# One layer's expert attention: the pair-matrix products of two tiles taken at once, and the copies around them moved

## What is computed

```python
gate_v = _get_sel_gate(x, sel_v_w, rs)      # sigmoid of logits, the best 2 of 8, normalised
gate_o = _get_sel_gate(x, sel_o_w, rs)
q = jnp.einsum('bsd,hpd->bhsp', x, q_w.reshape(H, P, D))
k = jnp.einsum('bsd,hpd->bhsp', x, k_w.reshape(H, P, D))
xv = jnp.einsum('bsd,hedp->bshep', x, v_w.reshape(H, E, D, P))
v = jnp.einsum('bshep,bshe->bhsp', xv, gate_v)
att = jax.nn.softmax(jnp.einsum('bhqp,bhkp->bhqk', q, k) * SCALE, axis=-1)
ctx = jnp.einsum('bhqk,bhkp->bqhp', att, v)
weighted = ctx[:, :, :, None, :] * gate_o[..., None]
out = jnp.einsum('bshep,hepd->bsd', weighted, o_w.reshape(H, E, P, D))
```

## Time and profile before

| what | value |
|---|---|
| median of 3 runs | 3170.46 us (3169.66 to 3173.8) |
| profiled execution, device time | 3168.74 us |
| its span | 3167.0 us |
| PE busy | 2907.0 us, 92% |
| DVE busy | 2780.7 us, 88% |
| ACT busy | 2341.8 us, 74% |
| POOL busy | 2322.8 us, 73% |
| chain that ended last | PE 59%, of it 46% in the units (L2221) and 3% in the pair products (L2254) |

### The profile page before, as it was taken

How to read it: one execution, slowest core, us unless ns; L and a number is a source line. 1 busy time by engine, 2 the same in 40 slices (tenths; PEclk the granted TensorE clock), 3 DMA queues, 4 the chain that set the end, 5 groups by cost and what they waited for, 6 DMA issues and landing times.

```text
span 3167.0 us, 78218 instructions
## 1 busy us (share of the span) xinstructions
PE 2907.0 (92%) x24620; PEld 2176.0 (69%) x24620; DVE 2780.7 (88%) x9085; ACT 2341.8 (74%) x7546; POOL 2322.8 (73%) x3112
## 2 busy tenths in 40 slices
PE   7489992897689996999999999999999999999998
PEld 7257762675357774677777777777777777777776
DVE  6789997899989986888888888898898898898897
ACT  4866668888976665777777777777777777777776
POOL 2799994666876662677777777777777777777777
PEclk8589995898789997999999999999999999999999
DMA  4000000220000004100000000000000000000000
GB/s 131 8 2 2 2 2 18 68 75 13 1 6 16 16 16 109 30 9 8 7 9 8 7 9 8 7 9 8 7 9 8 8 9 8 7 9 8 7 8 6
DMA packets 114508, 55.31 MB, mean 17 GB/s; under 512 B 18352, under 2 KB 113712, under 8 KB 114096
## 3 DMA queue, kind: packets, MB, share of 16 engines
q1 hardware_dynamic: 114096, 50.30, 5.8%
HBM read 41.81 MB, written 8.45 MB: 16 GB/s over the span
## 4 chain that ended last, share of the span: by engine, by line
PE 59%; DVE 1%; ACT 1%; POOL 1%; DMA 0%; issue 0%; SPq 0%; POOLq 0%; ACTq 0%; DVEq 0%
PE ps_sw_a L2221 24%; PE ps_sw_d L2221 22%; PE ps_sw_w L2267 4%; PE ps_sw_w L2254 3%; PE ps_sw_s L2236 2%; PE ps_sw_s L2278 2%; PE ps_sw_m L2243 1%; ACT sw_scaled L1962 0%; DVE sw_v_part L2117 0%; PE ps_sw_m L2229 0%; DMA sw_v<-in_L_ffn_v_w 0%; POOL sw_v_pair L1889 0%; DVE sw_v_low L2056 0%; DVE sw_o_low L2063 0%; ACT sw_v_high L2017 0%
## 5 line engine op out<-in xcount | busy, mean ns | idle before, releaser
L1962 ACT ACTIVATE sw_scaled<-ps_sw_a,sw_gate_o 128x128 f32<-128x128 f32 x2048 | 620.3, 447 | 254.1 <-PE ps_sw_a L2221 247.0
L1962 ACT ACTIVATE sw_scaled<-ps_sw_a,sw_gate_v 128x128 f32<-128x128 f32 x2048 | 597.3, 448 | 196.2 <-PE ps_sw_a L2221 194.4
L2117 DVE SCALAR_TENSOR_TENSOR sw_o_part<-ps_sw_d,sw_gate_o,sw_o_part 128x128 f32<-128x128 f32 x1920 | 555.6, 339 | 63.1 <-PE ps_sw_d L2221 60.5
L1889 POOL TENSOR_TENSOR sw_v_pair<-sw_v_part,sw_scaled 128x256 f32<-128x256 f32 x512 | 381.9, 746 | 157.0 <-DVE sw_v_part L2117 91.6
L2117 DVE SCALAR_TENSOR_TENSOR sw_v_part<-ps_sw_d,sw_gate_v,sw_scaled 128x128 f32<-128x128 f32 x1024 | 303.9, 337 | 126.1 <-PE ps_sw_d L2221 107.1
L1915 POOL TENSOR_TENSOR sw_o_rest<-sw_o_rest,sw_scaled 128x256 f32<-128x256 f32 x384 | 285.4, 743 | 158.0 <-ACT sw_scaled L1962 120.7
L2117 DVE SCALAR_TENSOR_TENSOR sw_v_part<-ps_sw_d,sw_gate_v,sw_v_part 128x128 f32<-128x128 f32 x1024 | 304.8, 339 | 0.0
L1918 POOL TENSOR_TENSOR sw_o_rest<-sw_o_rest,sw_scaled 128x256 f32<-128x256 f32 x384 | 282.6, 736 | 30.1
L1894 POOL TENSOR_TENSOR sw_v<-sw_v_pair 128x128 f32<-128x128 f32 x512 | 244.6, 478 | 40.1
L1014 POOL TENSOR_TENSOR at_key_wide<-at_keyT,c_half_heads 128x1024 f32<-128x1024 f32 x128 | 242.6, 1895 | 4.6 <-ACT at_keyT L1112 4.6
L2221 PE MATMUL ps_sw_a<-sw_v_high,sw_xT_high 128*128 128x512 f32 x512 | 234.5, 458 | 8.2 <-DVE sw_v_low L2056 8.2
(11 more groups left out here) (337 smaller groups left out, 8511.3 us busy)
## 6 DMA issues: line engine op xcount, KB each, us to landing
re_values<-in_ctx SPq DMA_DIRECT2D x128, 64.0 KB, 2.4
l_ctx<-in_ctx SPq DMA_DIRECT2D x16, 256.0 KB, 4.5
x<-in_x SPq DMA_DIRECT2D x16, 256.0 KB, 4.6
re_ctx<-in_ctx SPq DMA_DIRECT2D x16, 256.0 KB, 3.1
scratch_x<-x SPq DMA_DIRECT2D x64, 64.0 KB, 1.5
sw_x<-scratch_x SPq DMA_DIRECT2D x64, 64.0 KB, 1.9
sw_x_res<-scratch_x SPq DMA_DIRECT2D x64, 64.0 KB, 1.8
out<-sw_y SPq DMA_DIRECT2D x64, 64.0 KB, 1.5
```

Source lines behind the costliest of these rows:

```text
L1889: pool.tensor_tensor(v_pair[:, h % 2], v_part[:, h], scaled[:, h % 4, 2:4], ALU.add)\
L1962: act.activation(scaled[:, h % 4, e], ps_a[h % 2][:, e], ACT.Copy, scale=gates[:, s, h, HALF_E + e:HALF_E + e + 1]).then_inc(a_scaled[kind ...
L2117: dve.scalar_tensor_tensor(out=acc[:, e % 2], in0=ps_d[h % 2][:, e], scalar=gates[:, s, h, e:e + 1], in1=before, op0=ALU.mult, op1=ALU.add ...
```

## The change

- `pair_keys` now handles two tiles at once: the moving operand is 256 columns, `xT` of an even tile and of the next. `xT` holds 4 tiles and `uT` two. The step runs for even tiles only (`of_pair`). Of its four groups of two heads, groups 0 and 1 (`pair_keys(0)`, lag 2) come at the end of an iteration, groups 2 and 3 (`pair_keys(2)`, lag 3) between v4 and v5. Nothing of it is left between v5 and v6.
- The copies `keep_u` are four, each of 512 columns, for even tiles only; they follow v2, v3, v5 and v6.
- `xT_high` is made from `xT` in SBUF by a step of its own, `round_x`, with lag 3; `keep_x` keeps lag 1.
- All other lags of what follows grow by two (units v from 2 to 4, units o from 3 to 5, logits, route, scores and exp from 1 to 3, store from 4 to 6). `round_v`, `low_v`, `round_o`, `low_o` and the fetches of the weights keep theirs.
- The steps of `route` write over their inputs, and `place` is one row of 8 values read for all 16 groups.

```diff
-xT = k.sb("sw_xT", [P, 2, P])
+xT = k.sb("sw_xT", [P, 4, P])
...
-uT = k.sb("sw_uT", [P, SH, P])
+uT = k.sb("sw_uT", [P, SH, 2, P])
...
-place = k.sb("sw_place", [P, 2 * SH, SE])
+place = k.sb("sw_place", [P, SE])
...
-r = {n: k.sb("sw_r_" + n, G) for n in ("plus", "p", "eq1", "w1", "sel1", "p2", "eq2", "w2", "sel2", "sel")}
+r = {n: k.sb("sw_r_" + n, G) for n in ("equal", "sel", "p2")}
...
+def of_pair(step):
+    def at(i, s, rd):
+        if i % 2 == 0:
+            step(i, s, rd)
+    return at
...
     def _(sp):
...
-        sp.dma_start(place[:], A["c_place"].rearrange("p (g e) -> p g e", e=SE)).then_inc(q["place"], 16)
+        sp.dma_start(place[:], A["c_place"][:, 0:SE]).then_inc(q["place"], 16)
...
         def tile_in(dst, i):
...
-        straight([(0, fetch), (1, only_first(fetch_v)), (1, only_first(fetch_o(0, 4))), (2, fetch_residual),
-                  (2, only_first(fetch_o(4, 10))), (3, only_first(fetch_o(10, 16))), (4, store)])
+        straight([(0, fetch), (1, only_first(fetch_v)), (1, only_first(fetch_o(0, 4))), (4, fetch_residual),
+                  (2, only_first(fetch_o(4, 10))), (3, only_first(fetch_o(10, 16))), (6, store)])
...
-            pool.tensor_tensor(xT_low[:, s], xT[:, s], xT_high[:, s].bitcast(F32), ALU.subtract)\
+            pool.tensor_tensor(xT_low[:, s], xT[:, i % 4], xT_high[:, s].bitcast(F32), ALU.subtract)\
...
         def add_v(h):
...
-        stages = [(2, add_v(0)), (2, add_v(1)), (1, low_x), (4, finish)] + [(2, add_v(h)) for h in range(2, SH)]
-        stages += [(3, add_o(h)) for h in range(6)] + [(0, rstd)] + [(3, add_o(h)) for h in range(6, SH)]
+        stages = [(4, add_v(0)), (4, add_v(1)), (3, low_x), (6, finish)] + [(4, add_v(h)) for h in range(2, SH)]
+        stages += [(5, add_o(h)) for h in range(6)] + [(0, rstd)] + [(5, add_o(h)) for h in range(6, SH)]
...
         def keep_x(i, s, rd):
...
+            if not first(i, 4):
+                act.wait_ge(q["scores"], i - 3)
+                act.wait_ge(q["xT_low"], i - 3)
+            act.activation(xT[:, i % 4], ps_m[:, 0], ACT.Copy).then_inc(q["xT"], 1)
+        def round_x(i, s, rd):
+            act.wait_ge(q["xT"], i + 1)
...
-                act.wait_ge(q["scores"], i - 1)
...
-            act.activation(xT[:, s], ps_m[:, 0], ACT.Copy).then_inc(q["xT"], 1)
-            act.activation(xT_high[:, s], ps_m[:, 0], ACT.Copy).then_inc(q["xT_high"], 1)
+            act.activation(xT_high[:, s], xT[:, i % 4], ACT.Copy).then_inc(q["xT_high"], 1)
...
         def keep_probs(i, s, rd):
...
         def keep_u(n):
             def step(i, s, rd):
...
-                if n == 0 and not first(i, 1):
+                if n == 0 and i:
...
-                act.activation(uT[:, 4 * n:4 * n + 4], ps_w[n].rearrange("p (h t) -> p h t", h=4), ACT.Copy)\
-                    .then_inc(q["uT"], 1)
-            return step
+                act.activation(uT[:, 2 * n:2 * n + 2], ps_w[n % 2].rearrange("p (h c t) -> p h c t", h=2, c=2),
+                               ACT.Copy).then_inc(q["uT"], 1)
+            return of_pair(step)
...
         def keep_ctx(b):
             def step(i, s, rd):
...
-        exps = [(1, lambda i, s, rd, lo=lo: exp_scores(i, s, rd, lo)) for lo in range(0, SH, 2)]
-        vs, os = ([(lag, scale(kind, h)) for h in range(SH)] for kind, lag in (("v", 2), ("o", 3)))
-        stages = vs[:2] + [(1, keep_x)] + vs[2:4] + [(1, exp_logits), (2, keep_probs)] + vs[4:6]
-        stages += [(1, keep_u(0)), vs[6], (1, keep_u(1)), vs[7]] + os[:3] + [(2, keep_ctx(0)), os[3], exps[0]]
-        stages += [os[4], (2, keep_ctx(1)), os[5], exps[1], os[6], exps[2], os[7], exps[3]]
+        exps = [(3, lambda i, s, rd, lo=lo: exp_scores(i, s, rd, lo)) for lo in range(0, SH, 2)]
+        vs, os = ([(lag, scale(kind, h)) for h in range(SH)] for kind, lag in (("v", 4), ("o", 5)))
+        stages = vs[:2] + [(1, keep_x), (3, round_x), vs[2], (3, keep_u(0)), vs[3], (3, keep_u(1)), (3, exp_logits), (4, keep_probs)]
+        stages += [vs[4], vs[5], (3, keep_u(2)), vs[6], (3, keep_u(3)), vs[7]] + os[:3]
+        stages += [(4, keep_ctx(0)), os[3], exps[0], os[4], (4, keep_ctx(1)), os[5], exps[1], os[6], exps[2], os[7], exps[3]]
...
             def step(i, s, rd):
+                p = decays
...
-                    lambda: dve.tensor_scalar(r["plus"][:], decays[:], 1.0, None, ALU.add),
-                    lambda: dve.reciprocal(r["p"][:], r["plus"][:]),
...
+                    lambda: dve.tensor_scalar(p[:], decays[:], 1.0, None, ALU.add),
+                    lambda: dve.reciprocal(p[:], p[:]),
+                    lambda: dve.tensor_reduce(rm["m1"][:], p[:], AX.X, ALU.max),
+                    lambda: dve.tensor_tensor(r["equal"][:], p[:], wide(rm["m1"][:]), ALU.is_equal),
+                    lambda: dve.tensor_tensor(r["equal"][:], r["equal"][:], place[:].unsqueeze(1).broadcast_to(G), ALU.mult),
...
-                 for kind, lag in (("v", 2), ("o", 3)) for h in range(SH)}
-        R = [[(1, route(n))] for n in range(RANK)]
+                 for kind, lag in (("v", 4), ("o", 5)) for h in range(SH)}
+        R = [[(3, route(n))] for n in range(RANK)]
...
-            "v": [[], [], [(2, sums(0))], [(2, sums(1))], [(2, sums(2))], [], *R[0:5], R[5] + R[6], R[7],
+            "v": [[], [], [(4, sums(0))], [(4, sums(1))], [(4, sums(2))], [], *R[0:5], R[5] + R[6], R[7],
...
-            "o": [R[12], R[13] + R[14], R[15] + R[16], [(1, peak)], [(1, shifts)], R[17], R[18],
-                  [(2, low_ctx(0))], [(0, front(0))], R[19] + [(0, front(1))], [(0, front(2))],
-                  [(2, low_ctx(1))], [], [], [], []],
+            "o": [R[12], R[13] + R[14], R[15] + R[16], [(3, peak)], [(3, shifts)], R[17], R[18],
+                  [(4, low_ctx(0))], [(0, front(0))], R[19] + [(0, front(1))], [(0, front(2))],
+                  [(4, low_ctx(1))], [], [], [], []],
...
         def turn_x(i, s, rd):
...
-            if not first(i, 1):
-                pe.wait_ge(q["decays"], i)
+            if i >= 1:
+                pe.wait_ge(q["xT"], i)
+            if i >= 3:
+                pe.wait_ge(q["decays"], i - 2)
...
         def turn_probs(i, s, rd, lo):
...
         def logits(i, s, rd):
...
-            pe.wait_ge(q["xT_high"], i + 1)
-            pe.matmul(ps_m[:, 1], xT[:, s], W["sel"][:], start=True, stop=True).then_inc(q["logits"], 1)
-        def pair_keys(n):
+            pe.wait_ge(q["xT"], min(i + 3, TILES))
+            pe.matmul(ps_m[:, 1], xT[:, i % 4], W["sel"][:], start=True, stop=True).then_inc(q["logits"], 1)
+        def pair_keys(lo):
             def step(i, s, rd):
-                if i == 0:
-                    pe.wait_ge(prep["kept"], 2 + n)
-                elif not first(i, 2):
-                    pe.wait_ge(q["ctx_low"], 2 * (i - 2) + n + 1)
-                else:
-                    pe.wait_ge(q["uT"], 1 + n)
-                for h in range(4):
-                    m = pe.matmul(ps_w[n][:, h * P:(h + 1) * P], W["pair"][:, 4 * n + h], xT[:, s],
-                                  start=True, stop=True)
-                m.then_inc(q["u"], 1)
-            return step
+                if lo == 0:
+                    pe.wait_ge(q["xT"], i + 2)
+                for n in (lo, lo + 1):
+                    if n >= 2:
+                        pe.wait_ge(q["uT"], 2 * i + n - 1)
+                    elif i == 0:
+                        pe.wait_ge(prep["kept"], 3)
+                    else:
+                        pe.wait_ge(q["ctx_low"], 2 * (i - 2) + n + 1)
+                    both = xT[:, i % 4:i % 4 + 2].rearrange("p c t -> p (c t)")
+                    for h in range(2):
+                        m = pe.matmul(ps_w[n % 2][:, 2 * h * P:2 * (h + 1) * P], W["pair"][:, 2 * n + h], both,
+                                      start=True, stop=True)
+                    m.then_inc(q["u"], 1)
+            return of_pair(step)
...
         def context(i, s, rd):
-            upto = min(i + 2, TILES) if isinstance(i, int) else i + 2
-            wait_alone(pe, (q["v"], SH * i + SH), (q["p_kept"], i + 1), (q["uT"], 2 * upto))
-            if isinstance(i, int) and i == TILES - 1:
+            wait_alone(pe, (q["v"], SH * i + SH), (q["p_kept"], i + 1))
+            if i % 2 and i < TILES - 1:
+                pe.wait_ge(q["uT"], 2 * (i + 3))
+            elif i:
...
+            else:
+                pe.wait_ge(q["uT"], 4)
...
         def scores(i, s, rd):
-            waits = [(q["uT"], 2 * i + 2)]
+            waits = [(q["uT"], 4 * (i // 2) + 4)]
...
-                m = pe.matmul(ps_s[t], xT[:, s, t], uT[:, :, t], start=True, stop=True)
+                m = pe.matmul(ps_s[t], xT[:, i % 4, t], uT[:, :, s, t], start=True, stop=True)
...
-        vs, os = ([(lag, unit(kind, h)) for h in range(SH)] for kind, lag in (("v", 2), ("o", 3)))
-        turns = [(2, lambda i, s, rd, lo=lo: turn_probs(i, s, rd, lo)) for lo in (0, 4)]
```

(7 more changed lines are left out.)

21 lines of the change are left out of this document (9 added, 12 removed).

## The result

The changed kernel takes 3243.52 us, median of 4 runs (3242.52 to 3250.57); the kernel before took 3171.94 beside it. The ratio is 1.0231 [1.0213, 1.0248]: 2.3% slower, about 72 us. The forecast was 3217 us with a range of 3185 to 3248. Sign and mechanism held. The size did not: of 72 us some 45 were foreseen.

What follows compares the result with a forecast made beforehand. PE had no visible gap, with DVE back to back from v3 to o1. Profiled 3168.74, +39 us (31 pairs at +1.26), +8 for the start, and 1.7 to the median gave 3217 us, range 3185 to 3248.

Steps and rivals of the forecast that it cites:

- the third rival: All at upper ends: no DVE gain from POOL, ACT holds DVE up; 1.6 + 0.84 - 0.04 per pair, 3255 us; 7%.
- Saved on PE, 0.04 per pair: Pair product on PE: two wide products take 3.48 us per two tiles where four narrow ones took 3.52.
- the rival with the weight load: Pair product: weight load sets the price, a 256-column record costs 0.11 us, a product 0.88; 3165 us; 5%.
- Bare iteration, +1.1: Iteration without product before v5 and v6: PE reaches o0 early and waits for DVE; +1.1 us, ends 0.8 and 1.6.
- POOL would start at the end of the mix, some 0.15 to 0.2 us sooner: Bare iteration, v6: with ACT ahead, POOL's sum starts sooner and DVE's L2136 ends that much sooner.
- the reserve: At o0, before the change: DVE ends the mix of v6 0.45 us before PE writes the same bank.
- Filled iteration, +0.4: Iteration with 1.74 us of product before v5: DVE idles there, is late at o0; +0.4 us, ends 0 and 0.84.
- End of the bare iteration, -0.2: Around v0 and v1: the product behind o7 gives DVE and ACT time; -0.2 us, ends 0 and -0.3.
- The start, +8: First iterations: the one with both unit kinds begins later but is 3.2 us shorter; +8 us, between -1 and +14.
- Small edits at nothing: DVE's in-place route steps and one-row place keep number and width of instructions; put at nothing.
- ACT's order not added: keep_u(1) before exp_logits moves it by at most 0.61 us, less than DVE's 0.84 at v5; not added.
- DVE on time: Between v5 and v7: new timing parts two slow DVE steps from POOL's sums, DVE wins 1.06 us; 3163 to 3172; 10%.

Runs made afterwards that it cites:

- the runs with one and with both moved: The kernel before with DVE's moments and last route steps earlier: 3166.57 us; with ACT's exponentials one unit later: 3162.53 us; with both: 3159.53 us.
- the spread kernel: The changed kernel, wide product and lags kept, its four groups spread ahead of v5 and v6 in every iteration: 3174.41 us, ratio 1.0019.

## Why the prediction was right, and what it missed

The time lies in the range, 4.5 us below its upper end. It lies outside the forecast's own bounds of 3190 to 3240; the room above them had been left for the third rival. So the direction and the place were foreseen, and that the time still fell inside is in part luck.

- **Saved on PE, 0.04 per pair:** right, 0.07 measured. A 256-column record takes 0.215 us for 0.2175 assumed, so the rival with the weight load fell. The Trainium skill, "TensorE: Matmul & The Clock Gate", section "LDWEIGHTS (loading the stationary operand)", puts a load at its columns divided by 1.2 in ns, an estimate of 107 ns for 128. The trace agrees with that (two such loads start 0.11 us apart, last section), and not with the rival's step from it, that the load bounds these records; the run with halved width shows no difference.
- **Bare iteration, +1.1:** right in mechanism and place, measured 1.53, near the upper end of 1.6. The step "POOL would start at the end of the mix, some 0.15 to 0.2 us sooner" failed: POOL starts 0.14 us behind the end of the mix in both kernels (2066.52 to 2066.66 before, 2140.92 to 2141.06 here). It had been waiting for the mix all along, though the row of before named ACT: ACT's rows of v6 ended at 2065.57 there, 0.95 ahead of the mix. And L2148 takes 0.81 as L2136 did. Without that gain the term is 1.31. To it come 0.05, since PE's matmul starts that much behind the end of the mix (2140.92, 2140.97) and the reserve was counted to its end, and 0.11 for the restart behind o0; some 0.06 are not told apart. The restarts at v6 and v7 cost nothing of their own, since PE waits again at o0.
- **Filled iteration, +0.4:** DVE's delay was right, 0.89 for 0.84. The wait is 0.58 for 0.41 and the restart 0.11, 0.69 together. The handover of 0.06 (2111.39 to 2111.45) and the restart stood in no term, DVE was 0.05 later and PE some 0.06 sooner than counted.
- **Not foreseen: the context,** 0.38 per pair. The prediction stopped at o0. DVE's lateness goes on through v7's mix and POOL's last sum to the next reader.
- **End of the bare iteration, -0.2:** -0.32 there (3.01 for 3.33) and -0.03 at the end of the filled one, a little beyond the end of -0.3. Both DVE and ACT hold PE there, as the prediction said and the runs with one and with both moved show. That the product finds `low_ctx` done "well before" is true in the loop and not in iteration 4, where it waited 1.50 us.
- **The start, +8:** 12.8, inside the bounds of -1 to +14, but by two errors that partly cancel, which is luck. Iteration 4 began at 1270.05, 1265.9 without the 4.2 from ahead, at the early end of what was counted; and it took 30.02 us for the 18 assumed. It was not bound by DVE (19.75 us busy): the context waited 3.94 us for POOL, the product waited and ran at the clock's lower level. A row of before hinted at it: 30.55 us for value units alone, with the blocks beside them, at a granted clock of 0.73. The second weights' blocks explain 2 us at most.
- **Small edits at nothing, ACT's order not added:** right (1.0001; 4 us).
- **The rivals:** "DVE on time" did not come about; L2144 and L2148 kept 0.81 us. The sum per pair, 2.16 us, lies near the third rival's 2.40. Its first condition came true, since DVE gained nothing from POOL's earlier start; ACT held DVE up by 0.48 us at exp_logits, but that was worth only 0.18 a pair; the context and the restarts it did not name.

In sum 26 us were missed in loop and end (64.8 for 39) and 5 in the start. From iteration 6 on there are 29.5 pairs, not 31: 29.5 x 2.16 = 64 us. The 4.2 from ahead of this attention stood in no term either; the profiled run lies 7 us above the median.

## What to carry to other kernels

When two engines need nearly the same time for a stretch, a piece of work that only one of them does can be a spacer: its place decides, and its size may hardly do. Here 49 us hung on which side of one unit four matmuls stood, and leaving half of them out gave nothing. So before joining such pieces into fewer and larger ones, see whether each of them fills a wait, and follow a delay past the first waiting instruction to the engine behind the late one. Where removing one wait changes nothing, look for a second engine that holds the same buffer's neighbour, and move both.

## What was not expected of the hardware

- Behind a record for which PE had to wait, the next one starts 0.34 us later and not 0.23: 0.11 us for each restart, at v6, v7 and o0 alike. The weight loads show why. Around o0 of the bare iteration:

```profile
2139.74 0.19 PEld L2233 LDWEIGHTS ps_sw_a<-sw_o_high,sw_ctx_low 128*128 128x128 f32 x1
2140.97 0.19 PEld L2233 LDWEIGHTS ps_sw_d<-sw_o_high,sw_ctx_high 128*128 128x128 f32 x1 [1.04 <-DVE sw_v_part L2128]
2141.08 0.19 PEld L2233 LDWEIGHTS ps_sw_d<-sw_o_low,sw_ctx_high 128*128 128x128 f32 x1
```

Undisturbed, a load starts with the record before its own: 2139.74 for the record at 2139.97. The load of the waiting record waits too and starts at 2140.97, and the next one 0.11 later, which is just what the restart costs. No run removed it to test this.

- Scores of 256 columns in 8 records took as long as of 512 columns in 4: 1.02 us in the spread kernel (2047.74 to 2048.76) and 1.01 in the kernel before (2067.77 to 2068.78).
- DVE's steps with two operands in SBUF took 0.81 for 0.27 us when POOL's sum had just begun, in the kernel before, the changed one and five of the others. The Trainium skill, "SBUF — State Buffer", section "Who interferes with whom", has DVE instructions with two SBUF inputs contend with GpSimd instructions that read SBUF, over ports that one of them holds alone, and the trace agrees: L2148 starts at 2141.14, 0.08 behind POOL's sum, and ends 0.15 behind its end.
